# Eight places for the adj blocks of the first stage, and row sums halved on VectorE before TensorE folds them

## The reference, cut to what matters

```python
h = jnp.maximum(_layernorm(x), 0.0)
D = jnp.sum(adj, axis=1)
d_inv_sqrt = jnp.power(D + 1e-09, -0.5)
adj_norm = adj * d_inv_sqrt[:, None] * d_inv_sqrt[None, :]
x = x + relu((adj_norm @ h) @ W.T + b)
h = jnp.maximum(_layernorm(x), 0.0)
x = x + second_layer(h)     # relu(adj @ h @ gcn_w + gcn_b), layernorm, a Mamba block with a scan over 8192 rows
```

## Time and profile before

| | us |
|---|---|
| median of 3 runs | 2634.03 |
| lowest, highest | 2629.68, 2637.1 |
| the profiled execution | 2630.88 |
| its span in the trace | 2629.1 |
| busy in the span: PE / DVE / ACT / POOL | 2242.3 / 2075.4 / 978.3 / 1067.6 |
| stage A, from the trace | 0 to about 761 |
| stage B | to about 1397 |
| stage C | to the end |

### The profile page before, as it was taken

One profiled execution on the slowest core, in us unless ns is written; L12 is line 12 of the kernel. 1 busy time (PEld: TensorE's weight loads), 2 busy tenths in 40 slices (PEclk: granted clock), 3 DMA queues, 4 the chain that ended last, 5 costly groups with the idle time before them and its releaser, 6 DMA issues.

```text
span 2629.1 us, 21933 instructions
## 1 busy us (share of the span) xinstructions
PE 2242.3 (85%) x6864; PEld 1272.3 (48%) x6864; DVE 2075.4 (79%) x2079; ACT 978.3 (37%) x1696; POOL 1067.6 (41%) x461
## 2 busy tenths in 40 slices
PE   0347889999999999999999988888989888886776
PEld 0222444444448888888885434444434443443333
DVE  7889988887536666666653599999999999999997
ACT  0100000000015555554552455555545554555552
POOL 0000000000000000000000399999999999998554
PEclk9968889999999999999999999999999999997898
DMA  9999999889766665565547656565556565651221
GB/s 391 396 423 417 419 405 385 357 365 364 253 243 235 220 215 213 200 216 195 194 163 273 228 208 224 209 216 208 212 206 221 203 224 194 216 209 64 73 73 52
DMA packets 108323, 643.00 MB, mean 245 GB/s; under 512 B 14224, under 2 KB 15024, under 8 KB 42672
## 3 DMA queue, kind: packets, MB, share of 16 engines
q1 hardware_dynamic: 92160, 604.02, 60.6%
q10 hardware_dynamic: 16048, 37.57, 4.0%
HBM read 625.28 MB, written 16.25 MB: 244 GB/s over the span
## 4 chain that ended last, share of the span: by engine, by line
PE 54%; DVE 24%; DMA 9%; issue 8%; ACT 3%; DVEq 0%; SPq 0%; ACTq 0%
PE ps L841 21%; PE ps L759 14%; DMA ring<-adj 9%; PE ps L881 9%; DVE ps L677 7%; DVE arena L692 5%; DVE arena L584 4%; PE ps L959 3%; DVE ring L692 3%; PE ps L910 2%; PE ps L902 1%; DVE parts L718 1%; PE ps L963 1%; PE ps L921 1%; DVE arena L726 1%
## 5 line engine op out<-in xcount | busy, mean ns | idle before, releaser
L452 POOL TENSOR_TENSOR rstd<-base,minus_half 128x8 f32<-128x8 f32 (+1 forms) x40 | 84.7, 2117 | 1422.4 <-DVE base L504 813.2
L841 PE MATMUL ps<-adj_parts,h_parts 128*128 128x512 f32 x2592 | 593.4, 390 | 2.9 <-ACT adj_parts L1055 1.9
L881 PE MATMUL ps<-ring,diag_h 128*128 128x512 f32 x1152 | 562.1, 623 | 0.9 <-DVE arena L664 0.9
L584 DVE TENSOR_TENSOR arena<-arena,ring 128x2048 f32<-128x2048 f32 x208 | 476.9, 2293 | 90.8 <-DMA ring<-adj 79.1
L841 PEld LDWEIGHTS ps<-adj_parts,h_parts 128*128 128x128 f32 x2592 | 484.7, 188 | 109.1 <-ACT adj_parts L1055 5.0
L759 PE MATMUL ps<-ring,arena 128*128 128x512 f32 x928 | 433.4, 627 | 59.0 <-DMA ring<-adj 58.9
L692 DVE TENSOR_TENSOR_SCAN arena<-arena,state,ps 128x512 f32<-128x512 f32 x312 | 382.4, 1267 | 29.5 <-ACT arena L1130 9.7
L468 POOL TENSOR_TENSOR arena<-arena 128x1024 f32<-128x1024 f32 x156 | 377.5, 2431 | 67.7 <-ACT state L1122 67.6
L881 PEld LDWEIGHTS ps<-ring,diag_h 128*128 128x128 f32 x1152 | 228.0, 200 | 251.7 <-issue 246.8
L601 DVE TENSOR_TENSOR adj_parts<-ring,adj_parts 128x1024 fp32r<-128x1024 f32 x216 | 264.0, 1224 | 94.7 <-ACT adj_parts L1055 84.1
L1130 ACT ACTIVATE arena<-arena,a_sb 128x512 f32<-128x512 f32 x512 | 338.3, 708 | 0.4
(11 more groups left out here) (93 smaller groups left out, 1970.2 us busy)
## 6 DMA issues: line engine op xcount, KB each, us to landing
ring<-adj SPq DMA_DIRECT2D x480, 1024.0 KB, 6.7
arena<-c_scratch SPq DMA_DIRECT2D x128, 512.0 KB, 4.1
diag_h<-adj SPq DMA_DIRECT2D x32, 1024.0 KB, 12.4
arena<-x ACTq DMA_DIRECT2D x16, 512.0 KB, 6.0
x_scratch<-arena ACTq DMA_DIRECT2D x8, 512.0 KB, 3.0
arena<-x_scratch ACTq DMA_DIRECT2D x16, 256.0 KB, 5.0
out<-arena ACTq DMA_DIRECT2D x16, 256.0 KB, 3.8
lower_scratch<-arena ACTq DMA_DIRECT2D x7, 512.0 KB, 2.9
```

The source lines that it names most:

```text
L584: nc.vector.tensor_tensor(acc, acc, v, ALU.add).then_inc(adds_done, 1)
L841: last = nc.tensor.matmul(acc[:, c, :], h_parts[:, blk % 2, layer, h_part, a * F:(a + 1) * F], adj_parts[:, buf, adj_part, c * MM:(c + 1) ...
L881: last = nc.tensor.matmul((acc_c if i else y_ps)[:, c, :], tile_of(h1, JT * s + a), blk[:, a * STRIP + c * MM:a * STRIP + (c + 1) * MM], s ...
```

## The change

The places of the ring in stage A become eight (`RING_A`). The eighth is not in `ring` but in `arena`, which grows by one strip for it (`eighth`, behind the buffers of stage A); `slot_block` gives the tile of a place. Stages B and C keep seven and five places, and start in another place of the ring than before, since the place of a load follows from the one before it. After the last add of a strip, VectorE adds the right half of `rowacc` to its left half, 1024 columns, and counts `rows_summed`; the fold waits for that and has 8 matmuls instead of 16.

```diff
 RING = 7
+RING_A = RING + 1
 RING_C = 5
-ARENA = 24 * STRIP + 8
+ARENA = 25 * STRIP + 8
...
-        slot = (slot_of[-1] + 1) % (RING_C if phase == "C" else RING) if slot_of else 0
+        slot = (slot_of[-1] + 1) % {"A": RING_A, "B": RING, "C": RING_C}[phase] if slot_of else 0
...
         l1_stage = work(STRIP)
+        eighth = work(BLOCK)
...
+        def slot_block(slot):
+            return ring[:, slot, :] if slot < RING else eighth
...
-                sp.dma_start(ring[:, slot_of[q], :], adj[s, i]).then_inc(ring_in[slot_of[q]], 16)
+                sp.dma_start(slot_block(slot_of[q]), adj[s, i]).then_inc(ring_in[slot_of[q]], 16)
...
                     nc.vector.tensor_tensor(acc, acc, v, ALU.add).then_inc(adds_done, 1)
+                dve.wait_ge(adds_done, total_adds)
+                nc.vector.tensor_tensor(acc[:, 0:STRIP], acc[:, 0:STRIP], acc[:, STRIP:BLOCK], ALU.add).then_inc(rows_summed, 1)
...
-                pe.wait_ge(adds_done, adds_per_strip * (i + 1))
+                pe.wait_ge(rows_summed, i + 1)
                 if i:
                     pe.wait_ge(h0_ready, i)
                 for t in range(TPS):
-                    for a in range(JT):
-                        last = nc.tensor.matmul(ps_deg[:, t:t + 1],
-                                                rowacc[i % 2][:, a * STRIP + t * P:a * STRIP + (t + 1) * P], ones[:, :],
-                                                start=a == 0, stop=a == JT - 1)
+                    col = t * P
+                    last = nc.tensor.matmul(ps_deg[:, t:t + 1], rowacc[i % 2][:, col:col + P], ones[:, :],
+                                            start=True, stop=True)
                 last.then_inc(fold_done, 1)
```

More of the change, by code:

```diff
@@ L283, in build @@
         weights_in = sem("weights_in")
-        ring_in = [sem(f"ring_in{i}") for i in range(RING)]
+        ring_in = [sem(f"ring_in{i}") for i in range(RING_A)]
         diag_in = [sem(f"diag_in{i}") for i in range(BPS)]
@@ L294, in build @@
         adds_done = sem("adds_done")
+        rows_summed = sem("rows_summed")
         blocks_done = sem("blocks_done")
@@ L551, in arrived @@
                         dve.wait_ge(ring_in[slot_of[q]], 16 * turn_of[q])
-                        return ring[:, slot_of[q], :]
+                        return slot_block(slot_of[q])
                     dve.wait_ge(diag_in[q], 16 * (i + 1))
@@ L600, in low_part @@
                 dve.wait_ge(hi_ready, r + 1)
-                nc.vector.tensor_tensor(adj_parts[:, buf, 1, :], ring[:, slot_of[q], a * STRIP:(a + 1) * STRIP],
+                nc.vector.tensor_tensor(adj_parts[:, buf, 1, :], slot_block(slot_of[q])[:, a * STRIP:(a + 1) * STRIP],
                                         adj_parts[:, buf, 0, :].bitcast(F32), ALU.subtract).then_inc(lo_ready, 1)
@@ L872, in c_products @@
                     q = load_at["C", i, s]
-                    blk = arrived(q) if (a, c) == (0, 0) else ring[:, slot_of[q], :]
+                    blk = arrived(q) if (a, c) == (0, 0) else slot_block(slot_of[q])
                     first, last_s = s == rows_of[i][0], s == rows_of[i][-1]
@@ L1054, in high_part @@
                     act.wait_ge(ring_in[slot_of[q]], 16 * turn_of[q])
-                nc.scalar.activation(adj_parts[:, buf, 0, :], ring[:, slot_of[q], a * STRIP:(a + 1) * STRIP],
+                nc.scalar.activation(adj_parts[:, buf, 0, :], slot_block(slot_of[q])[:, a * STRIP:(a + 1) * STRIP],
                                      ACT.Copy).then_inc(hi_ready, 1)
```

## The result

| | before | changed |
|---|---|---|
| median, us | 2633.34 (6 runs, 2629.68 to 2637.1) | 2612.03 (6 runs, 2611.66 to 2612.43) |
| profiled execution, us | 2630.88 | 2612.32 |
| start of `fold(4)`, us | 437.35 | 430.90 |
| start of stage B (first matmul with `w0t_sb`) | 762.35 | 746.41 |
| first scan work on VectorE | 1480.44 | 1464.37 |

The changed kernel run a second time, on another occasion, gave 2613.68 us (5 runs) and a ratio of 0.9932 (0.992 to 0.9944), so the two give a gain of 18 to 21 us, and the intervals overlap.

What follows compares the result with a forecast made beforehand. DMA was taken to bound stage A up to strip 4, TensorE from `fold(4)` on. 6.3 us at `fold(4)`, partly in slow time, with 5.3 from later folds gave 10.1: profiled 2620.8, median 2624, range 2616 to 2632.

Steps and rivals of the forecast that it cites:

- rival 1: Stage A: the eighth place moves no data earlier; sum 4.2 to 5.8 us, time 2629, chance 0.19.
- rival 3: Strip 5, after longer idle: TensorE stays at 1.2 GHz, slower than before; 2645 if until `diagonal(4)`; chance 0.05.
- the sum of 10.1 us: Stage A from `fold(4)` on: total time saved there, including 5.3 us from the three later folds.
- start of `fold(4)`: Strip 4: last add at 432.8 instead of 437.30 us, plus 1.33 us for the new add, so start at 434.2.
- length of `fold(4)`: Strip 4: half as many matmuls halve the fold from 6.28 to 3.14 us.
- products behind it (clock): Behind `fold(4)`: part of the 6.3 us gained falls in slow time, counted as +1.5 us.
- folds 5 to 7: Later strips of stage A: folds halved to 1.86, 1.73 and 1.73 us without a wait, 5.3 us saved.
- clock behind `fold(6)`: From 632 us: a half-long fold may avoid the 0.59 clock; counted at nothing, 1.6 us in the range.
- the size of the DMA gaps: Stage A up to 394 us: eight places recover 1.9 us in strip 1 and 2.6 in strip 3, bounds 0 and 5.5.
- Folds 0 to 3: DMA-bound half of stage A: their 3 us each reach nothing, since VectorE and the DMA engines are ahead.
- rule of the Trainium skill: Ahead of `fold(4)`: idle of 5.2 us instead of 3.91 could bring slow time sooner or more often, costing half of itself.
- rival 2: Stage A: the clock helps, 6.3 + 5.3 + 1.6 = 13.2 us, time 2621, chance 0.12.

Runs made afterwards that it cites:

- The eighth place alone: Changed kernel with the add of the halves taken out and the fold of before, eight places kept: 2623.88 us, ratio 0.9966 to the kernel before.
- without the add: Changed kernel with the add of the halves left out, the short fold summing only the left half: 2611.63 us, ratio 0.9919 to the kernel before.
- long late: Changed kernel with the fold's 8 matmuls each issued twice in strips 4 to 7 alone: 2625.72 us, ratio 0.9975 to the kernel before.
- the add alone: Changed kernel with seven places in stage A, keeping the add of the halves and the fold of 8 matmuls: 2624.03 us, ratio 0.9962 to the kernel before.
- before again: The kernel before, unchanged, run and traced a second time: 2633.8 us, 2629.52 to 2637.26 over 12 runs.
- turned: The kernel before with stages B and C starting one place further on in the ring, seven places in stage A: 2631.77 us, ratio 0.9998.
- doubled: Changed kernel with each of the fold's 8 matmuls issued twice in all strips: 2629.36 us, ratio 0.9985 to the kernel before.
- long early: Changed kernel with the fold's 8 matmuls each issued twice in strips 0 to 3 alone: 2615.53 us, ratio 0.995 to the kernel before.
- AHEAD 11, 10 and 9: Changed kernel with the diagonal one, two and three lower blocks earlier than with 12: 2610.04, 2607.94 and 2610.08 us.

## Why the prediction was wrong

The mechanisms were those of the prediction, and its rival 1 and rival 3 fell. Its sizes were too small, nearly all on one side. Against the sum of 10.1 us, in the pair of profiled executions:

| term | predicted, us | measured, us |
|---|---|---|
| start of `fold(4)` | -3.2 | -6.45 |
| length of `fold(4)` | -3.1 | -2.7 |
| products behind it (clock) | +1.5 | +0.5 |
| folds 5 to 7 | -5.3 | -5.6 |
| clock behind `fold(6)` | 0 (-1.6 as an extra) | -1.7 |
| stage A | -10.1 | -15.9 |
| last stage | 0 | -2.5, within the spread of executions |
| median against the profiled execution | 0 | -2.7 |

Of the 11.2 us by which the forecast fell short, 5.8 lie in stage A. Nearly all the rest, 5.2, belongs to the last stage and to the place of the two profiled executions among their runs, and the second run of the changed kernel shows a gain 3 us smaller.

**The step that failed is the start of `fold(4)`, and in it the size of the DMA gaps.** The prediction read them from the share of time in which the DMA engines were busy: 1.9 us in strip 1, none in strip 2, 2.6 in strip 3, 4.5 together, with 5.5 as the upper bound. It had the sizes by the rate beside them, 3.5 and 3.0 us, and didn't use them. The eighth place alone makes `fold(4)` start 5.9 us earlier than in the first trace of before, and 6.5 earlier than in the second. Summed over all stretches up to 400 us, the changed kernel has moved 166.16 MB and the kernel before 163.55, which is 2.6 MB or, at 424 GB/s, 6.2 us; the second traces give 166.44 and 163.38 MB, 7.2 us. Of the 6.2 us, 1.1 MB (2.7 us) come between 120 and 140 us, 0.35 MB (0.8 us) between 220 and 260, where strip 2 has its diagonal, 1.0 MB (2.3 us) between 320 and 340, and 0.1 MB before all that. So strip 1 was sized too low by 0.8 us. Strip 2 was left out, because its share was 1.02 and 1.00 while its rate was down to 387 and 371 GB/s in two stretches of the kernel before:

```profile
236.00:240.00 4.00, 4.00 (x11) 1.75 (x10) 3.79 (x3) 0.00 (x0) 0.00 (x0) 1.00 1.02 387
240.00:244.00 4.00, 1.41 (x4) 0.34 (x2) 3.09 (x2) 0.00 (x0) 0.00 (x0) 0.95 1.00 371
```

How the sum divides differs between executions. In the other three traces with seven places strip 2 lacks 0.1 MB at most, and strip 3 lacks 1.4 to 1.8 MB against the first trace of the changed kernel (3.2 to 4.2 us), where the first one lacks 1.0. The share of idle time shrank by 4.6 us only. `diagonal(3)` started 6.6 us earlier in the first pair and 7.1 in the second, close to what the bytes say.

Another 1.1 us came behind it: from the issue of the last diagonal load of strip 4 to its landing it took 12.73 us for 13.82.

```profile
421.16 13.82 DMA diag_h<-adj
```

With the add of 1.24 us against it, the 7.7 us make the 6.45 measured. The runs show what this goes with. With AHEAD 12 that time is 12.7 to 12.9 us in the five traces with short folds in strips 0 to 3 (changed twice, without the add, long late, the add alone) and 13.8 to 14.2 us in the six with long ones (before, before again, turned, the eighth place alone, doubled, long early), with seven places as with eight. So it comes with the short early folds and not with the place, and it is why the add alone doesn't start `fold(4)` later. By what way a fold of strip 0 to 3 reaches these loads isn't shown.

**The clock behind long folds was counted at nothing.** The prediction saw it and gave it 1.6 us as an extra with little chance. It goes with a fold of 32 records: in six traces with folds that long in strips 5 to 7 (before, before again, turned, eighth place alone, doubled, doubled late) there is a granted clock below 0.9 in or right behind one or two of them, with no idle of TensorE ahead. In the seven traces with the short fold in strips 5 to 7 and eight places (changed twice, without the add, long early, AHEAD 11, 10 and 9) there is none behind folds 5 to 7 or anywhere from 452 to 1480 us, though with AHEAD 11, 10 and 9 TensorE idled 0.24 to 0.59 us ahead of `fold(5)`. Where the short fold has one behind it, in the run of the add alone, TensorE had idled 2.6 us. The price is 1.7 us in the first pair and 5.1 where it falls on two folds (the eighth place alone). It differs from execution to execution. The runs of kernels with long late folds spread over 4 to 10 us, those of the changed kernel over 0.8 and 1.6; that the one explains the other wasn't shown, since AHEAD 11 and 9, with short folds, spread over 5.5 and 4.3.

**The clock behind `fold(4)` came back sooner than predicted.** The prediction fixed its return at 11.0 us after the start of the fold, from two long folds. Worked out in the same way from the stretches, it returned 10.4 to 12.8 us after the start in the six traces with a long `fold(4)`, but 5.8 to 9.4 us after it in the eight with a short one: 9.4 and 6.5 in the two of the changed kernel. The loss is 5.1 or 6.8 us with the long fold, and 1.7 to 5.1 with the short one. So here too the fold is worth more than its length.

**Folds 0 to 3 do reach something.** The prediction said that they lie in the half that the DMA bounds. Beside the diagonal loads of strip 4, `fold(0)` matters. It took 6.96 us and ended 0.3 us ahead of VectorE's `degree_base(0)` in the kernel before, at 102.75 against 103.01 us. The add alone pushes its start by 0.9 us, and with the long fold it is then late and opens the DMA gap again, as the runs with doubled early folds show; both ways together are worth 1.9 us in the median. The short fold pays here for the add, which the prediction missed.

**What held.** The add is 1.24 us long, lies in the idle ahead of the next strip's first add and costs only where `fold(4)` waits (about 1.1 us). `fold(5)` doesn't wait with eight places and waits with seven, by 2.6 us. The gap ahead of the diagonal loads stayed. The idle ahead of `fold(4)` was 4.08 us rather than 5.2, since the last diagonal add came 1.1 us sooner after `diagonal(3)` than before. By the rule of the Trainium skill that the prediction weighed ("TensorE: Matmul & The Clock Gate", section "HAM oscillation") a longer idle could have brought the slow time on sooner or more often. The idle hardly grew, so the change itself doesn't test that; over the fourteen traces the losses after 2.85 and after 5.30 us of idle are both 5.1 us, and the smallest, 1.7, follows the shortest idle, 1.48. The slow clock behind the long folds 5 to 7 had no wait of TensorE ahead of it, so that rule doesn't account for it.

The chance of 0.12 for rival 2 was too low and its time, 2621, too high: the clock's extra and the gaps as the bytes have them together give 10.1 + 1.6 + 1.7 = 13.4 us, the diagonal loads and the clock behind `fold(4)` 1.1 and 1.0 more. The rest up to the 21.3 us between the first medians is mostly spread: the later medians of before are 2631.6 to 2633.8 us and that of the changed kernel 2613.68.

## What to carry to other kernels

Measure a gap in the DMA by the bytes that are missing as well as by the share of busy time, and don't write off work ahead of the point where the bottleneck passes from one engine to another: here the length of the folds in the DMA-bound half still moved later transfers. A long row of one-column matmuls costs TensorE more than its length, since the products behind it may run at half clock; shorten it with an add on an engine that waits there anyway. A buffer more and a shorter reduction can each pay for what the other would break (here the wait of `fold(5)` and the gap of strip 1), so judge them together.

## What the runs showed of the hardware

The granted clock of TensorE fell with no idle at all ahead of it: in the kernel with doubled late folds TensorE was busy for 4.00 us of each of the stretches around `fold(6)`, and the clock was 0.88 and 0.70 in the two that follow its start at 622.40 us. The one-column matmuls of a fold take 3.6 us for 32 records at full clock and 7.0 at half, though their work on the array is a single column each. With the fold of 16 records, 1.84 us, the clock fell in these traces only where TensorE had waited 1.48 us or more. And a DMA share of 0.98 to 1.04 went with anything from 372 to 424 GB/s in the changed kernel's stretches shown above, so a share near 1 can hide an eighth of the rate.
